# A MetaFormer block with routed experts: the last weight transfer in two pieces, index searches ahead of the up products, gathers and scatters in turn

## What is computed

```
x = x + einsum('oc,bchw->bohw', W(V), ln_c(x))      # W: product of 32 Householder reflections
t = tokens(x);  xf = ln_t(t)                          # (4096, 128)
S = softmax(xf @ W_router + b_router)                 # (4096, 32)
G_ek, idx_ek = top_k(S.T, 128)                        # each of 32 experts picks its 128 best tokens
up = xf[idx_ek] @ W_up[group] + b_up[group]           # 8 groups of 4 experts, 128 -> 341
Eout = silu(up) @ W_down[e] + b_down[e]               # 341 -> 128
y.at[idx_ek].add(G_ek * Eout);  out = from_tokens(t + y)
```

## Time and profile before

| what | us |
|---|---|
| median of three runs | 200.35 |
| the profiled execution's own time | 198.85 |
| its span | 196.8 |
| TensorE matmul busy | 146.2 (74%) |
| GpSimd busy | 108.4 (55%) |
| VectorE busy | 91.1 (46%) |
| ScalarE busy | 71.0 (36%) |
| mean granted TensorE clock | 0.809 |

### The profile page before, as it was taken

How to read it: one execution, slowest core, us unless ns; L and a number is a source line. 1 busy time by engine, 2 the same in 40 slices (tenths; PEclk the granted TensorE clock), 3 DMA queues, 4 the chain that set the end, 5 groups by cost and what they waited for, 6 DMA issues and landing times.

```text
span 196.8 us, 2406 instructions
## 1 busy us (share of the span) xinstructions
PE 146.2 (74%) x697; PEld 89.2 (45%) x697; DVE 91.1 (46%) x407; ACT 71.0 (36%) x241; POOL 108.4 (55%) x118
## 2 busy tenths in 40 slices
PE   1999965723126213995999699999975999999990
PEld 0557855611105101452357236776662344444590
DVE  2454998984774861322464513221299022200550
ACT  3266999437894500321233132345400000000161
POOL 2027479986460027773766557687788778730000
PEclk9999998555555555557599859999996699999999
DMA  4999994336989952221212122243414333369996
GB/s 98 301 336 308 289 292 120 82 81 214 393 252 263 330 217 67 67 70 33 66 51 67 33 70 32 27 40 27 40 17 40 27 27 34 35 113 328 395 284 189
DMA packets 33502, 28.31 MB, mean 144 GB/s; under 512 B 6800, under 2 KB 27216, under 8 KB 33360
## 3 DMA queue, kind: packets, MB, share of 16 engines
q1 hardware_dynamic: 26769, 21.70, 37.5%
q0 software_dynamic: 5280, 4.33, 15.3%
q10 hardware_dynamic: 1440, 2.13, 3.3%
HBM read 17.53 MB, written 10.62 MB: 143 GB/s over the span
## 4 chain that ended last, share of the span: by engine, by line
PE 37%; POOL 21%; issue 14%; DVE 12%; DMA 9%; ACT 3%; another core or an unknown queue 1%; SPq 0%; POOLq 0%; DVEq 0%; ACTq 0%
POOL acc L502 8%; PE PT L1129 7%; PE PZ L1142 6%; PE PM L1129 6%; POOL rs L463 4%; DMA x<-acc 3%; PE PM L1142 3%; POOL rs L456 3%; PE PT L969 3%; DMA acc<-X,idx 2%; PE PZ L1169 2%; PE PT L1117 2%; POOL act L469 2%; DVE wdn L914 2%; POOL act L466 2%
## 5 line engine op out<-in xcount | busy, mean ns | idle before, releaser
L502 POOL DMA_INDIRECT acc<-X,idx x26 | 43.4, 1669 | 11.5 <-issue 9.3
L493 POOL DMA_INDIRECT xg<-token_rows,idx x32 | 30.5, 954 | 31.4 <-DVE idx L906 23.2
L904 DVE TENSOR_SCALAR_CACHE_REDUCE junk<-PZ,k 128x128 f16<-128x128 f32 x32 | 11.1, 347 | 24.8 <-PE PZ L1099 14.6
L1017 PE MATMUL PZ<-stage_w,X 128*128 128x192 f32 x64 | 16.2, 410 | 6.3 <-DVE act L749 5.8
L1142 PE MATMUL PZ<-wdn,act 128*128 128x128 f32 x132 | 18.2, 281 | 1.0 <-DVE X L945 1.0
L627 ACT ACTIVATE X<-PZ 128x512 f32<-128x512 f32 x4 | 2.4, 597 | 45.2 <-PE PZ L1169 45.2
L1129 PE MATMUL PT<-xgT,wup 128*128 128x512 f32 (+3 forms) x28 | 18.2, 740 | 0.0
L620 ACT ACTIVATE act<-PT,bup 128x512 f32<-128x512 f32 (+3 forms) x14 | 9.0, 640 | 24.3 <-PE PT L1129 20.9
L1017 PEld LDWEIGHTS PZ<-stage_w,X 128*128 128x128 f32 x64 | 13.4, 238 | 8.2 <-DVE act L749 7.4
L1142 PEld LDWEIGHTS PZ<-wdn,act 128*128 128x128 f32 x132 | 16.0, 191 | 2.4 <-DVE X L945 1.4
L1129 PE MATMUL PM<-xgT,wup 128*128 128x512 f32 (+3 forms) x26 | 16.2, 714 | 0.0
(11 more groups left out here) (172 smaller groups left out, 280.5 us busy)
## 6 DMA issues: line engine op xcount, KB each, us to landing
X<-in_x SPq DMA_DIRECT2D x8, 256.0 KB, 5.2
acc<-zero SPq DMA_DIRECT2D x4, 512.0 KB, 5.2
acc<-x SPq DMA_DIRECT2D x8, 256.0 KB, 4.2
token_rows<-xf SPq DMA_DIRECT2D x8, 256.0 KB, 3.6
xf<-acc ACTq DMA_DIRECT2D x8, 256.0 KB, 5.7
x<-acc SPq DMA_DIRECT2D x8, 256.0 KB, 7.2
out<-X SPq DMA_DIRECT2D x8, 256.0 KB, 3.1
wup<-in_L_ffn_W_up SPq DMA_DIRECT2D x1, 1364.0 KB, 7.8
```

The source lines that it names most:

```text
L493: nc.gpsimd.indirect_dma_start(out=xg[:, e, :], out_offset=None, in_=rows[:, :], in_offset=bass.IndirectOffsetOnAxis(ap=idx[:, e:e + 1], a ...
L502: nc.gpsimd.indirect_dma_start(out=acc[i][:, :], out_offset=bass.IndirectOffsetOnAxis(ap=idx[:, e:e + 1], axis=0), in_=eo[:, e, :], in_off ...
L904: link(nc.vector.tensor_scalar(junk2[:, :], PZ[:, e % 2, 0:P], c_("slot_col"), None, ALU.is_le, ALU.add, accum_out=below[:, e:e + 1]))
L1017: ins = mm(PZ[:, 2 * (g % 2) + u // 2, (u % 2) * W_:(u % 2 + 1) * W_], X[:, g, u * P:(u + 1) * P], stage_w[:, :], start=True, stop=True)
```

## The change

The last weight transfer (L405) is cut into one of 80 and one of 5 partitions, so five completions of 16 are waited for instead of four. The searches are put two by two ahead of each up product, the first twelve of them, and none ahead of down products; VectorE's order follows. GpSimd issues 20 gathers, then scatter 0, gather 20, scatter 1, gather 21 and so on to gather 31, and then the 14 scatters that are left.

```diff
+FR_EVEN = FR // 16 * 16
-AHEAD = E
+AHEAD = 20
 def finds_before_up(k, j):
-    downed = UNITS[k - 1][0] if k else 0
-    return min(E, FIRST_FINDS + downed + 3 * k + j + 1)
+    return min(E, FIRST_FINDS + 2 * (3 * k + j + 1))
 def finds_before_down(e):
-    ups = 3 * min(UNIT_OF[e] + 2, len(UNITS))
-    return min(E, FIRST_FINDS + e + ups + 1)
+    return min(E, FIRST_FINDS + 6 * min(UNIT_OF[e] + 2, len(UNITS)))
...
-            sp.dma_start(wdn2[0:FR, :, :], w_down[:, 2 * P:DFF, :].rearrange("e f c -> f e c")).then_inc(s_wdn, 16)
+            for f0, f1 in ((0, FR_EVEN), (FR_EVEN, FR)):
+                sp.dma_start(wdn2[f0:f1, :, :], w_down[:, 2 * P + f0:2 * P + f1, :].rearrange("e f c -> f e c")).then_inc(s_wdn, 16)
...
-            while AHEAD + 2 * e < E:
+            while AHEAD + e < E:
                 scatter(e)
-                gather(AHEAD + 2 * e)
-                gather(AHEAD + 2 * e + 1)
+                gather(AHEAD + e)
                 e += 1
...
                     e = e0 + q
-                    find_up_to(finds_before_down(e))
                     if e >= 3:
...
-            pe.wait_ge(s_wdn, 64)
+            pe.wait_ge(s_wdn, 80)
```

## The result

| | before | after |
|---|---|---|
| median of the runs made together | 201.07 us (199.31 to 204.23) | 203.94 us (201.5 to 204.43) |
| profiled execution, its span | 198.85, 196.8 us | 203.51, 201.5 us |

The account below looks back on a forecast made before the run. Two chains, GpSimd's scatters and TensorE's products, end together, and after the change TensorE's sets the end. Gather 31 -3.2, clock +2.6, wait for sums -0.46 give -1.0 us: 197.8 profiled, 199.3 us as median, range 195.2 to 202.6.

Parts of the forecast that it names:

- Which chain ends last: At the final transposes: GpSimd's scatter chain gets 15 us to spare, TensorE sets the end, only 0.46 us gained there.
- Part 1: Weight transfer in 80 and 5 partitions, at 289 GB/s: first gather moves from 72.20 to 67.9, 4.3 us earlier.
- Part 2: Searches ahead of up products: no added work, and the gathers' waits for indices (23.2 us idle) taken away.
- Part 3: GpSimd's gathers and scatters in turn: 3.10 us a pair, no gather waits, gather 31 lands at 131.9.
- rival (b): Scatters waiting for products hold up gathers: gather 31 lands at 134.5 or later, 202.4 us; chance 0.14.
- Part 3's baseline: TensorE's 58.65 us to the last unit's transposes, ending at 130.8, so about 1.1 us of waiting for gather 31.
- The clock: TensorE's wait for gather 31 lowers its clock and slows the three up products of unit 8: +2.6 us.
- rival (a): TensorE's clock holds: 196.7 us, or 193.9 if L1164 also starts at the high level; chance 0.33.

Follow-up runs that it names:

- transfer_b: Kernel before with only the weight transfer cut into 80 and 5 partitions, on a late chip: 197.42 us, ratio 0.9844.
- p1_transfer: Kernel before with only the weight transfer cut into 80 and 5 partitions, no late stretch: 190.41 us, ratio 0.9871.
- p12_no_turn: Kernel after with all 32 gathers ahead of all scatters, transfer and searches as changed: 190.96 us, no ratio.
- columns_late: Kernel after with the 1 MB of column numbers loaded only after the last index: 198.04 us, ratio 1.0291 against before.
- before_again: Kernel before unchanged, run and traced once more on a late chip: 201.37 us, ratio 1.0065.
- turn_only: Kernel before with only the GpSimd order changed, 20 gathers and then scatter and gather in turn: 205.73 us, ratio 1.0276.
- first11_old_28_c: Kernel after with the old search order, 11 searches first and 28 gathers ahead, second measurement: median 199.68 us, no ratio.
- ahead24: Kernel after with 24 instead of 20 gathers ahead of the turns: 196.81 us, ratio 0.9808 against before.
- ahead28: Kernel after with 28 instead of 20 gathers ahead of the turns: 197.59 us, ratio 0.9881 against before.
- search_only: Kernel before with only the searches moved, two ahead of each of the first twelve up products: 205.41 us, ratio 1.0251.
- filled_waits: Kernel after with 28 unread products on TensorE ahead of the waits of units 7 and 8: 204.81 us, ratio 1.0213 against before.

## Why the prediction was wrong, step by step

- **Which chain ends last: right.** Freeing GpSimd's scatter chain gained nothing (last scatter 5.5 us earlier, final transposes 5.2 us later), and the end was TensorE's.
- **Part 1: right in effect, its rate wrong.** -3.6 us at the first gather for -4.3 forecast (transfer_b and p1_transfer: -3.0 and -3.4). It makes the kernel 1.6% faster by itself on a late chip (transfer_b), 1.3% in p1_transfer. The 80 partitions moved at about 171 GB/s, not 289.
- **Part 2, "Added work: none", failed.** The step priced the searches by their work and by when an index is needed; but on late chips the new order of the searches goes with a stretch of about 15 us instead of about 5. Alone it costs 2.5%. By this, expert 0's output came at 96.93 instead of the 88.4 that it was due (86.05 in p12_no_turn, without the stretch).
- **Part 3, "no gather waits, with 3 us in hand", failed.** This is the step that moved gather 31, and with it the kernel's time. The slack was 4.8 us for scatter 0 and 3.0 us for scatter 4; the output of expert 0 came 8.5 us late, and that of expert 4 at 112.11, 9.5 us late. The forecast never looked at expert 2, whose output came at 106.36 and stopped scatter 2. The two waits (3.92 and 3.33 us, where 0.30 is usual) are 6.7 of the 8.4 us by which gather 31 was late; the pitch of a pair, 3.18 for 3.10, is 0.9 over eleven pairs, and the late gather 19 is 0.8. That is rival (b) ("VectorE is stalled ... gather 31 lands at 134.5 or later"), which had 0.14: gather 31 landed at about 140.2. A "remote" wait of 5.06 us, longer than the slack of any step, stood in the trace of before unexplained; a chance of 0.14 was low for that, although nothing in that trace said that the wait would grow.
- **Part 3's baseline failed too.** "It started at 76.47 and took 58.65 us" was taken as TensorE's need, so that gathers in turn seemed to make it wait 1.1 us. Those 58.65 us held before's own late stretch and its low clock; the work takes 46.0 us (p12_no_turn) to 51.9 us (p1_transfer). At 5.85 us a unit against 12.7 us for four gathers in turn, GpSimd is the slower one, whatever the searches do: about 7 us lost where signals are in time, 2.8% alone on a late chip. This error did not shift the forecast for gather 31, which was the later condition in it anyway (131.9 against 130.8), but it hid that the turns only pay where before is held up by something else. The trace of before had the number: ahead of its last unit at 135.12, the transposes of the two units before stand at
```profile
123.43 0.60 PE L1117 MATMUL PT<-k,xg 128*128 128x128 f32 x4
129.28 0.60 PE L1117 MATMUL PT<-k,xg 128*128 128x128 f32 x4
```
  5.85 us apart, as in p12_no_turn. 4 x 3.10 = 12.4 against 5.85 would have shown that TensorE catches up with the gathers and then waits at every unit.
- **The clock: right in kind.** The stretch from unit 8 to the one-hot products is 1.8 us longer where +2.6 was forecast; the products behind it are 1.2 us shorter, which the forecast had only in rival (a). The forecast had the Trainium skill ("TensorE: Matmul & The Clock Gate", section "HAM oscillation — how this bites in real kernels") speak against waits between bursts; columns_late agrees (0.71 and 0.66 around its two waits), but the waits themselves cost more than the clock after them.

The parts do not add up: alone -1.6, +2.5 and +2.8%, together +1.1 to 1.7%. A likely reason, not tested by itself: a long late stretch holds TensorE up while GpSimd goes on gathering, so the two losses overlap. With 24 or 28 ahead TensorE no longer waits at unit 8 on late chips, and the kernel is 1.9 and 1.2% faster than before in spite of its new searches.

Shown: the searches alone and the turns alone each make the kernel slower on late chips, and the turns also where there is no late stretch. Not shown: what the late stretch is in the machine, why some chips have none, and whether TensorE's order itself or the unbroken row of gathers that comes with it sets its length.

## What to carry to other kernels

Before two producers are put in turn on one queue, compare their common pitch with the consumer's pitch in an undisturbed stretch (5.85 against 12.7 us a unit), not with the consumer's total time, which may hide stalls that move or vanish with the change. A wait that the profile can't attribute is a term of the sum: it has to be bounded like any unknown cost, and the slack of each step compared with it. The depth of a prefetch is a size to be varied: 24 or 28 gathers ahead instead of 20 turned a loss of 1.1 to 1.7% into a gain of 1.9 or 1.2% on late chips with nothing else changed.

## What was not expected of the hardware

- The median of the same kernel before is 194.8 and 195.2 us on two chips (single runs from 189.0 to 197.3) and 200.3 to 201.4 on others. The traces taken on the slower chips all have a stretch, somewhere between 81 and 100 us, in which results of TensorE reach ScalarE and VectorE up to 10 us after their recorded end, and those on the two faster chips have none. In after, three readings within it follow at steps of 2.1 us (87.68, 89.77, 91.88).
- On the late chips the first such stretch was 5 to 6 us in every kernel with the old searches and 8 of them ahead (before, before_again, turn_only, transfer_b), some 9 us with the old order and 11 ahead (first11_old_28_c), and 12 to 15 us in those with the new ones (after three times, ahead24, ahead28, search_only, filled_waits). Some kernels have further short ones behind it (search_only near 115 to 123, ahead24 near 103 to 108).
